# Attention score terms of a graph layer, packed into 32-row and 32-column strips of the array

## The reference

```python
h = jnp.einsum('bni,io->bno', x, W)              # split into 4 heads of 32
e_i = jnp.einsum('bhnd,hd->bhn', h, a1)
e_j = jnp.einsum('bhmd,hd->bhm', h, a2)
e = e_i[:, :, :, None] + e_j[:, :, None, :]
e = jnp.where(e > 0, e, LRELU_SLOPE * e)
e = jnp.where(adj[:, None, :, :] > 0, e, NEG_INF)
attn = jax.nn.softmax(e, axis=-1)
out = jnp.einsum('bhnm,bhmd->bhnd', attn, h)
```

## Time and profile before

| what | value |
|---|---|
| median of 3 runs | 708.86 us (708.76 to 709.89) |
| the profiled execution | 708.05 us |
| span from its first to its last instruction | 705.9 us |
| busy: PE, DVE, ACT, POOL | 660.1, 601.6, 524.4, 401.1 us |
| the four first layers, up to the last copy of h0T | about 332 us of the span |
| instructions | 13197 |

### The profile page before, as it was taken

One profiled execution on the slowest core, in us unless ns is written; L12 is line 12 of the kernel. 1 busy time (PEld: TensorE's weight loads), 2 busy tenths in 40 slices (PEclk: granted clock), 3 DMA queues, 4 the chain that ended last, 5 costly groups with the idle time before them and its releaser, 6 DMA issues.

```text
span 705.9 us, 13197 instructions
## 1 busy us (share of the span) xinstructions
PE 660.1 (94%) x4380; PEld 430.2 (61%) x4380; DVE 601.6 (85%) x1360; ACT 524.4 (74%) x962; POOL 401.1 (57%) x357
## 2 busy tenths in 40 slices
PE   3899999999999999974899999999999999999995
PEld 2678888888888888752455555555555545545552
DVE  3777877777877777666699999999999999999996
ACT  2678888888888888723588888777787777777774
POOL 4656666666666666521255555555555555555554
PEclk9999999999999999985899999999999999999998
DMA  5111111111111100000333333333333334333332
GB/s 154 31 32 31 31 32 31 32 32 31 31 31 31 31 17 2 2 0 2 64 65 64 62 61 60 74 73 68 71 62 74 75 75 75 61 76 73 68 70 74
DMA packets 114690, 35.82 MB, mean 51 GB/s; under 512 B 87680, under 2 KB 114624, under 8 KB 114624
## 3 DMA queue, kind: packets, MB, share of 16 engines
q1 hardware_dynamic: 113424, 34.79, 23.0%
q10 hardware_dynamic: 1200, 0.20, 0.2%
HBM read 9.80 MB, written 4.19 MB: 20 GB/s over the span
## 4 chain that ended last, share of the span: by engine, by line
DVE 36%; issue 10%; PE 3%; POOL 2%; ACT 1%; DMA 0%; DVEq 0%; POOLq 0%; SPq 0%
DVE h_parts L1297 12%; DVE cand L1304 7%; DVE t_parts L1289 6%; DVE r L1308 5%; DVE new L1293 4%; PE psum L50 3%; POOL h0T L1264 2%; DVE out L1280 2%; DMA h_nodes<-h_parts 0%; DVE h_parts L1299 0%; DVEq L1307 0%; ACT cand L1241 0%; POOLq L1046 0%; ACT t_parts L1233 0%; PE psum L1193 0%
## 5 line engine op out<-in xcount | busy, mean ns | idle before, releaser
L50 PE MATMUL psum<-h_parts,gru_w 128*128 128x512 f16 x720 | 185.1, 382 | 6.3 <-DVE out L1280 3.9
L1264 POOL TENSOR_TENSOR h0T<-cand,zh 128x512 f32<-128x512 f32 x80 | 101.6, 1270 | 143.4 <-DVE cand L1304 143.4
L50 PE MATMUL psum<-t_parts,gru_w 128*128 128x512 f16 x720 | 181.5, 379 | 0.0
L50 PEld LDWEIGHTS psum<-h_parts,gru_w 128*128 128x128 f16 x720 | 69.8, 98 | 91.9 <-issue 10.8
L1258 POOL TENSOR_TENSOR zh<-z,h0T 128x512 f32<-128x512 f32 x80 | 101.7, 1271 | 25.8 <-ACT z L1236 25.8
L50 PEld LDWEIGHTS psum<-t_parts,gru_w 128*128 128x128 f16 x720 | 66.9, 98 | 66.4 <-DVE t_parts L1289 2.9
L1233 ACT CAST t_parts<-psum 128x512 f16<-128x512 f32 x80 | 46.8, 585 | 72.6 <-PE psum L50 72.6
L1297 DVE CAST h_parts<-h0T 128x512 f16<-128x512 f32 x80 | 90.1, 1126 | 4.9 <-PEq L380 4.8
L578 POOL TENSOR_TENSOR prob<-prob,row_max 128x512 f32<-128x512 f32 x64 | 68.7, 1086 | 20.0 <-DVE row_max L956 18.7
L1241 ACT ACTIVATE cand<-new,gates_b 128x512 f32<-128x512 f32 x80 | 65.0, 812 | 7.4 <-DVE new L1293 7.3
L1236 ACT ACTIVATE z<-psum,gates_b 128x512 f32<-128x512 f32 x80 | 62.2, 778 | 5.9 <-PE psum L50 0.9
(11 more groups left out here) (131 smaller groups left out, 1202.5 us busy)
## 6 DMA issues: line engine op xcount, KB each, us to landing
x_all<-in_x SPq DMA_DIRECT2D x16, 256.0 KB, 3.2
adj<-in_adj SPq DMA_DIRECT2D x16, 256.0 KB, 2.8
out_x<-out SPq DMA_DIRECT2D x16, 256.0 KB, 2.3
h_nodes<-h_parts SPq DMA_TRANSPOSE x80, 3.1
gw<-in_L_gnn_weight SPq DMA_DIRECT2D x1, 320.0 KB, 5.7
W<-in_L_gnn_W SPq DMA_DIRECT2D x2, 128.0 KB, 4.4
wi<-in_L_gnn_w_ih SPq DMA_DIRECT2D x1, 192.0 KB, 5.7
wh<-in_L_gnn_w_hh SPq DMA_DIRECT2D x1, 192.0 KB, 4.4
```

Of the source, the lines that this page charges most:

```text
L50: return nc.tensor.matmul(out, lhsT, rhs, start=start, stop=stop)
L1264: pool.tensor_tensor(state(now), by_graph(cand[now.s][:, :]), by_graph(zh[now.s][:, :]), ALU.add)\
```

## The change

The e product becomes four products, one for each graph, with a weight of only 32 columns (`score_w` is 128 x 32: high terms in columns 0 to 7, the same in 8 to 15, the rest zero). Graph g's lands in partitions 32g to 32g + 31 of the bank, 128 columns, so that it uses its own 32-column strip of the array. ACT's copy and DVE's e_lo then work on 128 x 128 instead of 512 columns; e_lo adds e and `lo_rows` times the rounded e in one operation over all partitions, where the column `lo_rows` is -1 in the low rows and 0 in the others. The products of e_i and e_j read only the 32 rows of their graph, so that graph g uses row strip g and writes bank g. The order is new too: the four masks come first and need neither e_hi nor e_lo, then the four e_i products, then the sixteen e_j products, head by head over the graphs; `out_1` comes behind all of them. The pick tables are made at the start by two DVE sums over the identity and two ACT copies, no longer by POOL.

```diff
-LO_ROW = 32
+ROWS = 32
-        t["score_w"] = sb("score_w", [128, 128])
+        t["score_w"] = sb("score_w", [128, ROWS])
+        t["lo_rows"] = sb("lo_rows", [128, 1])
-    def pick_rows(self, pool):
...
+    def sum_rows(self, dve):
+        v, n = self.nc.vector, 2 * HEADS
+        dve.wait_ge(self.eyes, 2)
+        by_row = self.t["ident"][:, :].rearrange("p (g q k) -> p g q k", g=GROUP, q=ROWS // n)
+        v.tensor_reduce(self.row[:, :], by_row[:, :, 0:2, :].rearrange("p g q k -> p k g q"), AXIS.XY, ALU.add)\
+            .then_inc(self.rows, 1)
+        v.tensor_reduce(self.t["lo_rows"][:, :], by_row[:, :, 1, :], AXIS.XY, ALU.add).then_inc(self.rows, 1)
+        dve.wait_ge(self.rows, 2)
+        v.tensor_scalar(self.t["lo_rows"][:, :], self.t["lo_rows"][:, :], -1.0, None, ALU.mult).then_inc(self.rows, 1)
+    def pick_rows(self, act):
+        act.wait_ge(self.rows, 1)
+        for k, pick in enumerate((self.t["pick_i"], self.t["pick_j"])):
+            self.nc.scalar.copy(pick[:, :, :], self.row[:, k * HEADS:(k + 1) * HEADS].unsqueeze(2)
+                                .to_broadcast([128, HEADS, 128])).then_inc(self.picks, 1)
...
-        e_parts = two("e_parts", [128, COLS], F16)
+        e_high = one("e_high", [128, NODES], F16)
+        e_parts = two("e_parts", [128, NODES], F16)
...
-                mm(nc, P[:, B_EDGE, :], t["score_w"][:, :], hT[:, :]).then_inc(e_psum, 1)
+                for g in range(GROUP):
+                    last = mm(nc, P[g * ROWS:(g + 1) * ROWS, B_EDGE, 0:NODES], t["score_w"][:, :],
+                              hT[:, g * 128:(g + 1) * 128])
+                last.then_inc(e_psum, 1)
...
+            def mask(group, g):
+                if g == 0:
+                    pe.wait_ge(gone_ready, group.count)
+                    wait_users(pe, (x_attended, group.before(1)))
+                mm(nc, P[:, g, :].rearrange("p (h m) -> p h m", h=HEADS), t["identb"][:, :],
+                   gone[group.odd][:, g, :].unsqueeze(1).to_broadcast([128, HEADS, NODES]), True, False)
+            def scores(group):
                 pe.wait_ge(e_lo, group.count)
+                for g in range(GROUP):
+                    rows = slice(g * ROWS, (g + 1) * ROWS)
+                    mm(nc, P[:, g, :].rearrange("p (h m) -> p h m", h=HEADS), e_parts[group.odd][rows, :],
+                       t["pick_i"][rows, :, :], False, False)
                 for h in range(HEADS):
+                    for g in range(GROUP):
+                        rows = slice(g * ROWS, (g + 1) * ROWS)
+                        last = mm(nc, P[:, g, h * 128:(h + 1) * 128], t["pick_j"][rows, h, :],
+                                  e_parts[group.odd][rows, :], False, h == HEADS - 1)
+                        if h == HEADS - 1:
+                            last.then_inc(score_ready, 1)
...
-            a.copy(e_parts[group.odd][:, :], P[:, B_EDGE, :]).then_inc(e_hi, 1)
+            a.copy(e_high[:, :], P[:, B_EDGE, 0:NODES]).then_inc(e_hi, 1)
...
+                v.scalar_tensor_tensor(e_parts[group.odd][:, :], e_high[:, :], t["lo_rows"][:, 0:1],
+                                       P[:, B_EDGE, 0:NODES], ALU.mult, ALU.add).then_inc(e_lo, 1)
```

More of the change, by code:

```diff
@@ L279, in __init__ @@
         self.ones = sb("ones", [1, 128])
+        self.row = sb("row", [128, 2 * HEADS])
         self.loaded = sem("score_weights_loaded")
         self.eyes = sem("identities_made")
+        self.rows = sem("rows_made")
         self.picks = sem("picks_made")
@@ L365, in scale @@
                      t["gates_b"][:, E_UNSCALE:E_UNSCALE + 1])
-        for row in (0, LO_ROW):
+        for row in (0, 2 * HEADS):
             linked(v.tensor_scalar(t["score_w"][:, row:row + 2 * HEADS], self.was[:, :, :].rearrange("p k h -> p (k h)"),
@@ L595, in slot @@
             def slot(at, number):
-                if number == 1:
-                    score_weights.pick_rows(pool)
                 if number == 2:
@@ L656, in turn_adj @@
                 turn(B_HW, adj[group.odd]).then_inc(adjT_psum, 1)
-            def scores(group, g):
-                pe.wait_ge(gone_ready, group.count)
-                pe.wait_ge(e_hi, group.count)
-                pe.wait_ge(e_lo, group.count)
[L663 to L668, removed]
-                for h in range(HEADS):
-                    last = mm(nc, bank[:, h, :], t["pick_j"][:, h, :], e, False, h == HEADS - 1)
-                last.then_inc(score_ready, 1)
+            def mask(group, g):
[5 more added lines that the diff above has]
+            def scores(group):
+                pe.wait_ge(e_lo, group.count)
+                for g in range(GROUP):
+                    rows = slice(g * ROWS, (g + 1) * ROWS)
+                    mm(nc, P[:, g, :].rearrange("p (h m) -> p h m", h=HEADS), e_parts[group.odd][rows, :],
+                       t["pick_i"][rows, :, :], False, False)
+                for h in range(HEADS):
+                    for g in range(GROUP):
[4 more added lines that the diff above has]
+                            last.then_inc(score_ready, 1)
             def turn_prob(group, g):
@@ L733, in slot @@
                 if number == 1:
-                    pe.wait_ge(score_weights.picks, 1)
+                    pe.wait_ge(score_weights.picks, 2)
                     pe.wait_ge(score_weights.eyes, 4)
@@ L742, in slot @@
                 if at(1):
-                    scores(at(1), 0)
-                    scores(at(1), 1)
+                    mask(at(1), 0)
+                    mask(at(1), 1)
+                    mask(at(1), 2)
+                    mask(at(1), 3)
+                    scores(at(1))
                 if at(3):
@@ L747, in slot @@
                 if at(1):
-                    scores(at(1), 2)
-                    scores(at(1), 3)
                     turn_adj(at(1))
@@ L814, in keep_e @@
                 act.wait_ge(e_psum, group.count)
-                if group.before(2).exists:
-                    act.wait_ge(score_ready, group.before(2).graph_count(GROUP - 1))
-                a.copy(e_parts[group.odd][:, :], P[:, B_EDGE, :]).then_inc(e_hi, 1)
+                if group.before(1).exists:
+                    act.wait_ge(e_lo, group.before(1).count)
+                a.copy(e_high[:, :], P[:, B_EDGE, 0:NODES]).then_inc(e_hi, 1)
             def keep_hW(group):
@@ L911, in _ @@
             act.wait_ge(constants, 3)
+            score_weights.pick_rows(act)
             slots(act, slot)
@@ L950, in keep_e_lo @@
                 dve.wait_ge(e_hi, group.count)
-                v.tensor_tensor(e_parts[group.odd][LO_ROW:2 * LO_ROW, :], P[LO_ROW:2 * LO_ROW, B_EDGE, :],
-                                e_parts[group.odd][LO_ROW:2 * LO_ROW, :], ALU.subtract).then_inc(e_lo, 1)
+                if group.before(2).exists:
+                    dve.wait_ge(score_ready, group.before(2).graph_count(GROUP - 1))
+                v.scalar_tensor_tensor(e_parts[group.odd][:, :], e_high[:, :], t["lo_rows"][:, 0:1],
+                                       P[:, B_EDGE, 0:NODES], ALU.mult, ALU.add).then_inc(e_lo, 1)
             def row_max(group, g):
@@ L1033, in slot @@
                     add_out(at(2), 0, B_TURN)
+            score_weights.sum_rows(dve)
             slots(dve, slot)
```

## The result

The changed kernel takes 717.5 us (median of 4 runs, 717.1 to 719.2) against 709.0 us before: a ratio of 1.012, 95% interval 1.010 to 1.014. It is slower by 1.2%; 717.8 us was forecast, so the number came within 0.3 us. The profiled execution took 717.63 us, its span is 715.8 us (before: 708.05 and 705.9).

A forecast was written before the change was run, and what follows sets the result against it. PE and an ACT/DVE chain were both taken as tight, within 0.34 us. Terms 8.5 + 1.0 + 0.9 - 1.5 = +8.9 on 708.05 gave 717.0, plus 0.8 for the median: 717.8 us, range 709.5 to 733.

The forecast's parts named there:

- What bounds the kernel: Steady slot: PE at 99% and an ACT/DVE chain both tight, within 0.34 us of each other.
- The e product is worth 0 in a steady slot: Shortening 0.92 us of PE work gains 0, because the hidden product waits for ACT's copy of zT anyway.
- keep_e and e_lo: ACT's copy (0.60) and DVE's operation (0.68) shrink to 128 columns; both worth 0 in a steady slot.
- P: PE's score work beyond the four masks before leaky 0 can start: 0.78 us, between 0.45 and 1.78.
- The page's ratio for P: Skill page's 3.07x for four strips, applied to e_i and e_j: about 0.55 us, total some 5 us instead of 9.
- The steady slot: Leaky 0 0.99 us later, less 0.34 slack before the neighbour product: 0.65 us longer, 13 slots, 8.5 us.
- The start: Before the steady slots, shorter e product and copies on the path: 1.5 us off, between 0.6 and 2.0.
- Slots 2 and 16: Slots with little or no slack before the neighbour product: 0.99 us and 0.94 us longer.
- strips in turn: Rival: strips do not run abreast in the score products, 734 us; chance 0.11.
- PE is the bound after all: Rival: ACT absorbs the later leaky 0 before the neighbour product, slots follow PE's work, 682 to 686 us; chance 0.11.
- It cancels: Rival: steady-slot growth under 0.19 us offsets the gain at the start, total within 0.2%; chance 0.08.

The follow-up runs named there:

- e1: The kernel before with only the four masks moved first, e and score products left full-array: 712.7 us, ratio 1.005.
- e4: The changed kernel with another order on ACT alone, rstd of layer 1 before leaky 0 and the normalising activations before leaky 1: 707.5 us, ratio 0.998.
- e5: The kernel before with another order on ACT alone, rstd of layer 1 before leaky 0 and normalisation before leaky 1: 710.8 us, ratio 1.003.
- e2: The changed kernel with its strips, but scores issued graph by graph in the order of the kernel before: 730.8 us.
- e7: The changed kernel plus unread 512-column products, eight in slot 1 and four before the neighbour product in every slot with a group in layer 1: 714.35 us, ratio 1.008.

## Why the prediction was right, point by point

- **What bounds the kernel**: right. e1 shows it without any strip, e4 and e5 together show both sides of it: before the change PE's work and ACT's y are within 0.34 us of each other, relief of ACT alone (e5) gives nothing, and relief of PE pays only once ACT's y no longer waits for the scores (e4).
- **The e product is worth 0 in a steady slot**: right within 0.08 us. In the changed kernel hidden starts 1.83 after the neighbour product (before 1.81), with PE idle for 0.32 where e had been; in e2 1.74.
- **keep_e and e_lo**: 0.60 became 0.28 and 0.68 became 0.35, and no slot shows a gain; right.
- **P, the scores beyond the masks**: the term that was mis-sized. I took 0.78 (0.16 for emptying, 0.22, and 0.40 up to the 13th e_j product). The rows say 0.09 for the change of mode (0.96 from the first mask to the first e_i product, four masks being 0.87), 0.22 for e_i, and some 0.23 for e_j, since its 0.32 holds the change back, 0.09. Together 0.54, and leaky 0, 0.74 later, says 0.53. So the e_j products run fully abreast: that was the low end of my range, which I had set aside because no row showed pairs closer than 0.057.
- **The page's ratio for P.** The Trainium skill (TensorE: Matmul & The Clock Gate, Part 3) gives 3.07x for four strips at 512 columns. My estimate with that ratio for both kinds was about 0.55, closer than my 0.78, but in part by coincidence. By the rows of this case four e_i products of 512 columns take 0.22 to the next kind instead of 0.87, a quarter and so more than the page's gain, sixteen e_j with the change behind them 0.32 instead of 0.92; and the estimate had no term for a change of mode.
- **The steady slot**: 0.65 forecast, 0.345 measured. Leaky 0 is 0.74 later (not 0.99). ACT's own small gaps behind it took up 0.15, which I had not counted, so y is 0.59 later; the slack took 0.35, as forecast (4.45 against 4.05 + 0.05); and the neighbour product takes 1.09 to the next instead of 0.89, its first weight load, of y, starting with it and not 0.11 ahead as before, and ACT's copy of zT follows 1.20 behind its start instead of 1.09, which adds back 0.1. The sum, 0.34, is what the slots show.
- **The start**: -1.5 was forecast, and at the first mask of slot 2 the kernel is 1.2 behind. The e product there takes 0.59 instead of 1.84 (0.46 was forecast), and the first mask is 1.08 earlier, but slot 1 then runs at the lower clock. This step failed: I read the shorter PE work at the start as pure gain and had no term for the clock, although the rows had shown TensorE at half its speed in this very place: the same e product takes 1.84 there, 12.60 to 14.44, and 0.92 in a steady slot, 161.85 to 162.77.
- **Slots 2 and 16**: 0.99 and 0.94 were forecast, by the same P. Without the 0.44 of the clock slot 2 grew by 0.65, and slot 16 by 0.69.
- **The single long slot** (1.4) and the rest behind slot 16 (1.1) had no term. The first is the clock, the second for the most part, as far as the rows show; e7, whose long slot is gone, still has 1.2 behind slot 16, of which 0.69 is slot 16's own.
- **The rivals**: strips in turn fell with the first rows of the profile. "PE is the bound after all" fell with e1 and e7, where PE's work was unchanged or 9 us larger. "It cancels" needed P under 0.32, and P is 0.53.

The total came within 0.3 us of the forecast by luck, because two errors met: the steady slots cost 4 us less than forecast, and the clock some 4 us that were not in the sum (2.4 in slot 1, 0.4 in slot 2, 1.4 in the long slot). The direction and the mechanism in the steady slots are confirmed; the closeness of the number is not.

## What to carry to other kernels

Before packing small products, ask who reads the first result. To let the strips run abreast the products are grouped by kind, and what is put in front of the first result (here three more masks, 0.65 of 0.74 us) delays an engine that was fed graph by graph. Measure the slack at each hand-over between a busy engine and its consumer first; if both are tight, relieve both, here by moving the scores off ACT's path as well (1.2% lost became 0.2% won, and 0.5% with the spare products). And look at TensorE's clock when PE's work gets lighter: here it cost some 4 us that no term had foreseen.

## What the runs showed of the hardware

- Four 32-row strips into four banks run fully abreast: 16 products of 128 columns with their 16 weight loads take 0.32 us with the change of mode behind them, as long as 4 products in one strip (e2), against 57 ns each in turn before. One strip alone is no faster than a full product.
- A change between full products and row strips costs 0.09 us either way (e2: 0.31 against 0.22, and 0.32 against 0.23). The Trainium skill (TensorEngine Tiling (Array Packing), Key Properties) says that changing the mode drains the engine; the trace agrees that there is a cost, and sizes it at 0.09, below the 0.16 that I had taken from the pipelined length of a matmul.
- The clock column can't be trusted at the start of these traces. In e2 it reads 1.00 in this window, while in it a mask is 0.52 to 0.54 us ahead of its e_i product and that one 0.40 ahead of the e_j products, and 0.31 and 0.22 in a steady slot:

```profile
37.00:40.00 3.00, 2.97 (x13) 1.17 (x12) 1.47 (x10) 1.98 (x6) 1.04 (x1) 1.00 0.02 5
```

The spacing of matmuls of one kind is the better witness at the start of a trace.
